# Splitting the second layer's expert weights inside the first layer's expert loop

## The chip, the cores and the metric

One Trainium2 chip, one of its cores. The core has a matrix engine (TensorE, "PE" in the profile; its weight loads are "PEld"), a vector engine (VectorE, "DVE"), an activation engine (ScalarE, "ACT"), a general engine (GpSimd, "POOL") and SyncE ("SP"), which here only issues DMAs. The engines run their own instruction streams and meet through semaphores. The metric is the device time of one execution in microseconds (us), the median of several runs.

## What is computed

A two-layer tower over 8 images: a tokenizer, an attention block with fake quantization, a mixture of 8 experts (top 2), then a second attention block and a second mixture of 8 experts with a shared expert. 2048 tokens of width 192 in all. What matters here are the two expert layers, and of them the weights of the second:

```
def _L1_ffn_ref(x, Wr, W1, b1, W2, b2, sW1, sb1, sW2, sb2):
    logits = xf @ Wr.T
    topv, idx = jax.lax.top_k(logits, K)                      # K = 2 of E = 8
    gates = ...at[arange(T)[:, None], idx].add(softmax(topv))
    h = relu(einsum('td,ehd->teh', xf, W1) + b1)              # W1: 8 experts, 768 x 192
    y = einsum('teh,edh->ted', h, W2) + b2                    # W2: 8 experts, 192 x 768
    moe = einsum('te,ted->td', gates, y)
    return moe + 0.1 * K * (relu(xf @ sW1.T + sb1) @ sW2.T + sb2)
```

The float32 weights are used as two float16 parts, a high one and a low one: high = weight x scale rounded to float16, low = weight x scale - high. Making the two parts of a weight piece is called a split below. The scales are powers of two from the largest absolute weight of a matrix; those of the second layer's expert weights are known before the first expert layer begins.

## The kernel before

The program is a row of blocks; all engines meet at the end of each. Those that matter, in order: the first layer's expert preparation, its expert loop, and then the second attention in four blocks (projection, maxima, context, output), then the second expert layer.

**The expert loop** (`experts`, lines 2193 to 2452) works off 23 slots. A slot is a group of tokens of one expert: 7 small slots of 128 tokens come first, then 16 large slots of 256 (`BIG`, 16; `EARLY`, 7). Each engine has its order written out. In step p, PE does `up` of slot p+1 (L2282, 30 matmuls into `m_pu`), turns the gathered rows of slot p+2 (L2250, into `m_px`), and does `down` of slot p (L2301, 36 matmuls into `m_py`). `down` waits until DVE has made the low part of that slot's hidden values (`lowered`) and has taken the result of the slot before (`out`). ACT does for each slot three GELUs (L2379) and three high parts (L2368). DVE's step p is: copy of the turned rows of slot p+2 (L2404), three low parts of slot p+1 (L2412), result of slot p (L2422). POOL issues the gathers of later slots' rows (L2213) and the adding scatters of the results (L2225), both indirect DMAs. SP issues eight small loads, then waits for the last two scatters and fetches the first quarter of `h` back (`take_back`, L1598), on which the next block's first DVE work waits.

**The splits.** The second layer's expert weights are 16 pieces: for each of the 8 experts one of `w1` (128 x 1536 float32, 768 KB) and one of `w2` (128 x 1152, 576 KB). The class `Halves` (L2606) brings them through SBUF: `fetch` loads a piece into one of 4 places of `hv_raw`, a split makes both parts in one of 3 places of `hv_parts`, `store` writes them to DRAM (`w1h_d`, `w2h_d`), from where the second expert layer loads them (`load_halves`, L1740, which waits for the store of each piece). All of this stands in the second attention:

- Projection block (L2824 to L3068): pieces 0 to 5 (`FRONT`). ACT makes the high part (L2640) and a scaled copy (L2645), POOL subtracts (L2650). They stand in ACT's order ahead of and inside `take(i)`, whose copies (L2969) free the PSUM banks for which PE waits. At the end of the block POOL reduces the shared expert's weight maxima over the partitions (`weigher.reduce`, L193) and DVE computes the scales from it (`weigher.scales`, L201 to L204).
- Maxima block (L3158): nothing of it.
- Context block (L3231 to L3346): pieces 6 to 15. DVE makes both parts (L2657, L2659), two pieces ahead of the first image and one behind each of the 8 images.

## Time and profile before

| | us |
|---|---|
| median of 3 runs | 943.89 (942.99 to 946.34) |
| profiled execution, its own time | 942.19 |
| its span | 940.4 |
| PE busy | 680.5 |
| DVE busy | 655.0 |
| ACT busy | 639.8 |
| POOL busy | 309.9 |

Busy shares over the whole span hide that the stages have different limits, so the profile is read by stretch. The expert loop of the first layer runs from about 410 to 545 us of the span, the projection block from 552 to 614, the maxima block to 650, the context block to 702. In such a table "PEclk" is the clock granted to TensorE as a share of 2.4 GHz, and the DMA share is the mean busy share of the core's 16 DMA engines.

### The profile page before, as it was taken

The page shows a single profiled execution, that of the slowest core. Times are in us where ns is not written, and L with a number is a line of the kernel's source. Part 1 is how long each engine was busy: PE and PEld are TensorE (multiplying, and loading weights), DVE is VectorE, ACT ScalarE, POOL GpSimd, SP SyncE. Part 2 cuts the span into 40 slices and gives each one's busy share as a digit, 9 for nine tenths or more (in the row PEclk, how much of TensorE's full clock was granted, in tenths as well). Part 3 has the DMA queues.
Part 4 walks back from the last instruction along what each step waited for, and adds up shares of the span by engine and source line. Part 5 has one row for each costly group of instructions (what it writes and reads, how often), then busy time and mean ns, then how long its engine had stood idle before and what let it go on. Part 6 is the DMA issues. An engine that isn't in the chain of part 4 may idle for free. (4 is left out here: it accounts for less than half of the span.)

```text
span 940.4 us, 19693 instructions
## 1 busy us (share of the span) xinstructions
PE 680.5 (72%) x7374; PEld 518.0 (55%) x7375; DVE 655.0 (70%) x1370; ACT 639.8 (68%) x1217; POOL 309.9 (33%) x250
## 2 busy tenths in 40 slices
PE   2675472344199655989999937646965898999995
PEld 2553240122077423479999934334544467999994
DVE  3478998999679888855454558667669875554542
ACT  1468955999799686876556427788844752977672
POOL 6730650000000000047887443400001202688754
PEclk9797555555589776999999967955987899999999
DMA  6444772000032224943343365600744942333432
GB/s 200 144 89 116 245 243 61 0 17 9 1 105 100 93 84 141 333 106 68 61 60 54 33 188 190 235 2 28 267 184 159 331 177 73 60 63 61 62 34 30
DMA packets 61478, 106.06 MB, mean 113 GB/s; under 512 B 9725, under 2 KB 43144, under 8 KB 61144
## 3 DMA queue, kind: packets, MB, share of 16 engines
q1 hardware_dynamic: 45016, 88.48, 28.4%
q0 software_dynamic: 16384, 16.53, 11.3%
q8 instruction: 50, 0.82, 0.4%
q14 instruction: 28, 0.23, 0.1%
HBM read 77.20 MB, written 27.77 MB: 112 GB/s over the span
## 5 line engine op out<-in xcount | busy, mean ns | idle before, releaser
L2412 DVE SCALAR_TENSOR_TENSOR m_hT<-m_pu,m_unit,m_hT 128x512 f16<-128x512 f32 (+1 forms) x138 | 86.3, 663 | 21.2 <-ACT m_hT L2368 21.2
L1140 ACT ACTIVATE a_ex<-m_pieces,a_nb 128x256 bf16<-128x256 f16 x192 | 94.3, 492 | 5.4 <-DVE a_nb L1166 5.4
L2404 DVE COPY m_xgT<-m_px 128x768 f16<-128x768 f16 (+1 forms) x46 | 22.9, 497 | 102.6 <-PE m_px L2250 102.6
L2375 ACT ACTIVATE m_pu<-m_pu,m_b,m_unit 128x256 f32<-128x256 f32 (+1 forms) x138 | 63.7, 507 | 44.7 <-PE m_pu L2282 42.7
L979 PE MATMUL a_pp<-a_room 16*128 16x256 bf16 x240 | 56.1, 413 | 40.0 <-DVE m_pieces L1154 31.8
L2368 ACT ACTIVATE m_hT<-m_pu,m_unit 128x512 f16<-128x512 f32 (+1 forms) x138 | 81.3, 634 | 0.0
L2213 POOL DMA_INDIRECT m_xg<-xn_d,m_token x70 | 68.9, 985 | 35.1 <-issue 18.9
L2379 ACT ACTIVATE m_pu<-m_pu,m_unit 128x512 f32<-128x512 f32 (+1 forms) x69 | 41.2, 596 | 52.1 <-PE m_pu L2282 52.1
L2225 POOL DMA_INDIRECT out_h<-m_yo,m_token x39 | 62.1, 1592 | 31.4 <-DVE m_yo L2422 19.6
L2225 POOL DMA_INDIRECT h_d<-m_yo,m_token x39 | 62.1, 1591 | 25.6 <-issue 10.1
L2282 PE MATMUL m_pu<-m_xgT,m_pieces 128*128 128x256 f16 (+1 forms) x690 | 69.4, 260 | 0.9 <-DVE m_xgT L2404 0.9
L2282 PE MATMUL m_pu<-m_xgT,m_w 128*128 128x256 f16 (+1 forms) x690 | 69.1, 259 | 0.9 <-DVE m_xgT L2404 0.9
L979 PEld LDWEIGHTS a_pp<-a_room 16*128 16x128 bf16 x240 | 30.4, 136 | 65.7 <-DVE m_pieces L1154 39.0
L2282 PEld LDWEIGHTS m_pu<-m_xgT,m_pieces 128*128 x690 | 60.0, 100 | 6.8 <-DVE m_xgT L2404 1.2
L2282 PEld LDWEIGHTS m_pu<-m_xgT,m_w 128*128 x690 | 59.7, 99 | 6.8 <-DVE m_xgT L2404 1.3
L2301 PE MATMUL m_py<-m_w,m_hT 128*128 x702 | 63.0, 246 | 0.0
L2301 PE MATMUL m_py<-m_pieces,m_hT 128*128 x702 | 61.7, 246 | 0.9 <-DVE m_yo L2422 0.9
L2301 PEld LDWEIGHTS m_py<-m_w,m_hT 128*128 128x128 f16 x702 | 58.5, 98 | 0.0
L2301 PEld LDWEIGHTS m_py<-m_pieces,m_hT 128*128 128x128 f16 x702 | 57.7, 98 | 1.1 <-issue 1.1
L1154 DVE TENSOR_SCALAR m_pieces<-a_pp,a_sc 128x2048 f16<-128x2048 f32 x24 | 56.3, 2347 | 1.6 <-PEq L988 1.6
L1080 DVE TENSOR_REDUCE a_mxs<-a_pp 128x1 f32<-128x2048 f32 x24 | 53.0, 2283 | 2.2 <-PE a_pp L979 1.6
L1304 ACT ACTIVATE a_e<-a_pt 128x1024 f32<-128x1024 f32 x48 | 49.1, 1024 | 2.8 <-PE a_pt L1250 1.2
(494 smaller groups left out, 1675.6 us busy)
## 6 DMA issues: line engine op xcount, KB each, us to landing
m_pieces<-in_m_w SPq DMA_DIRECT2D x11, 768.0 KB, 5.1
a_early_w<-in_m_w SPq DMA_DIRECT2D x10, 768.0 KB, 5.4
hv_raw<-in_m_w SPq DMA_DIRECT2D x8, 768.0 KB, 7.1
w1h_d<-hv_parts SPq DMA_DIRECT2D x8, 768.0 KB, 4.0
m_w<-w1h_d SPq DMA_DIRECT2D x8, 768.0 KB, 8.7
m_pieces<-in_m_w SPq DMA_DIRECT2D x8, 576.0 KB, 6.1
a_room<-in_m_w SPq DMA_DIRECT2D x8, 576.0 KB
hv_raw<-in_m_w SPq DMA_DIRECT2D x8, 576.0 KB, 6.5
```

The costliest lines, as they stand in the source:

```text
L979: last = nc.tensor.matmul(pp[:, n % 2, j, qt * S:(qt + 1) * S], qkb[:, load % 2, h, qt * P:(qt + 1) * P], qkb[:, load % 2, H + h, :], star ...
L1080: v.tensor_reduce(mxs[:, n:n + 1], pp[:, n % 2], AX.XY, ALU.max, apply_absolute_value=True).then_inc(read, 1)
L1140: last = act.activation(ex[:, n % 2, r], v16t[:, n, r, :], ACT.Exp, bias=nbt[:, n, r:r + 1], scale=scale, accum_out=sumst[:, n, r:r + 1])
L1154: v.tensor_scalar(v16t[:, n], pp[:, n % 2].rearrange("p j (t q) -> p (j t) q", q=S), col["f_s"], HALF, ALU.mult, ALU.add).then_inc(read, 1)
L1304: act.activation(e[:, j], pt[:, j], ACT.Exp, scale=scale).then_inc(raised[j], 1)
L2213: pool.indirect_dma_start(xg[:, x.b, j, :], None, xn_d, bass.IndirectOffsetOnAxis(ap=token[:, n:n + 1], axis=0)).then_inc(got[x.b], 16)
L2225: pool.indirect_dma_start(total_d, bass.IndirectOffsetOnAxis(ap=token[:, n:n + 1], axis=0), yo[:, x.b, j, :], None, compute_op=ALU.add).th ...
L2282: last = nc.tensor.matmul(pu[:, u, q // 2, (q % 2) * w:(q % 2 + 1) * w], w1_bytes[:, bass.ds(e * (2 * W) + up_place(wpart, tail, q), 2 * P ...
L2301: last = nc.tensor.matmul(py[:, j * D:(j + 1) * D], hT[:, u, hpart, q * w + j * P:q * w + (j + 1) * P], w2_bytes[:, bass.ds(e * (2 * FC * ...
L2368: act.activation(hT[:, u, 0, n * 2 * w:(n + 1) * 2 * w], pu[:, u, n, 0:2 * w], ACT.Identity, scale=unit[:, 1:2]).then_inc(hhigh, 1)
L2375: act.activation(pu[:, u, n, q * w:(q + 1) * w], pu[:, u, n, q * w:(q + 1) * w], ACT.Relu, bias=b1[:, bass.ds(e * FC + 2 * n + q, 1)], sca ...
L2412: last = v.scalar_tensor_tensor(hT[:, u, 1, third], pu[:, u, n, 0:2 * w], unit[:, 1:2], hT[:, u, 0, third], ALU.mult, ALU.subtract)
```

## The change

All sixteen pieces are split in the first layer's expert loop by a new class `Ahead`, one behind each of the 16 large slots: ACT makes a high part behind each large slot's `hidden`, DVE the low part behind each large slot's `step`. The piece numbers follow the slots; even pieces are of `w1`, odd ones of `w2`. `Ahead` has one raw place and one place for the parts for each of the two kinds. Its `move` stands in SP's order between the small loads and the wait ahead of `take_back`. `Halves` keeps its code but has no pieces left (`COUNT` is 0), and `load_halves` waits for no store. The shared expert's `weigher.reduce` goes to POOL in the maxima block, and `weigher.scales` to DVE in the same block, behind pair 9 of 11.

```diff
@@ load_halves
-                    prepared.wait_put(sp, 2 * e + down)
+                    if 2 * e + down >= Halves.START:
+                        prepared.wait_put(sp, 2 * e + down - Halves.START)
@@ expert loop: sync, scalar, vector
                     if following:
                         following.load(sp)
+                        ahead.move(sp)
                         for p in (MAXT - 2, MAXT - 1):
                             sp.wait_ge(stored[p % 4], slot(p).landed)
                         take_back(c, total_d, back, sp, 0)
                     with act.Fori(0, BIG // 4) as k:
                         for n in range(4):
                             hidden(in_group(k, n))
+                            if ahead:
+                                ahead.split_high(act, k, n)
                     with dve.Fori(0, BIG // 4 - 1) as k:
                         for n in range(4):
                             step(in_group(k, n), in_group(k, n + 1), in_group(k, n + 2))
-                    steps(EARLY + BIG - 4, MAXT)
+                            if ahead:
+                                ahead.split_low(dve, k, n)
+                    for n in range(4):
+                        steps(EARLY + BIG - 4 + n, EARLY + BIG - 3 + n)
+                        if ahead:
+                            ahead.split_low(dve, BIG // 4 - 1, n)
@@ new
+class Ahead:
+    COUNT = 16
+    def __init__(self, c, a, scratch, ctx):
+        self.raw = c.sb("ah_raw", [P, 2, 2 * FF], F32, ctx)
+        self.parts = c.sb("ah_parts", [P, 2, 2, 2 * FF], F16, ctx)
...
+    def fetch(self, sp, n):
+        down = n % 2
+        if n >= 2:
+            sp.wait_ge(self.put[down], 16 * (n // 2))
+        sp.dma_start(self.tiles(down)[0], self.a["m1_w2" if down else "m1_w1"][n // 2])\
+          .then_inc(self.fetched[down], 16)
+    def store(self, sp, n):
+        down = n % 2
+        sp.wait_ge(self.low[down], n // 2 + 1)
+        sp.dma_start(self.scratch["w2h" if down else "w1h"][n // 2].rearrange("p (r w) -> p r w", r=2),
+                     self.tiles(down)[1]).then_inc(self.put[down], 16)
+    def move(self, sp):
+        for n in range(2):
+            self.fetch(sp, n)
+        for n in range(self.COUNT):
+            self.store(sp, n)
+            if n + 2 < self.COUNT:
+                self.fetch(sp, n + 2)
+        for down in range(2):
+            sp.wait_ge(self.put[down], 16 * (self.COUNT // 2))
+    def split_high(self, act, k, n):
+        act.wait_ge(self.fetched[down], k * 32 + 16 * (n // 2 + 1))
+        act.activation(parts[:, 0, :], raw, ACT.Identity, scale=scale).then_inc(self.high[down], 1)
+    def split_low(self, dve, k, n):
+        dve.wait_ge(self.high[down], k * 2 + (n // 2 + 1))
+        self.c.nc.vector.scalar_tensor_tensor(parts[:, 1, :], raw, scale, parts[:, 0, :], ALU.mult, ALU.subtract)\
+            .then_inc(self.low[down], 1)
@@ Halves
-    COUNT, FRONT, MIXED, RAW, PARTS = 2 * E, 6, 8, 4, 3
+    START = Ahead.COUNT
+    COUNT, FRONT, MIXED, RAW, PARTS = 2 * E - START, 0, 0, 4, 3
@@ projection block: gpsimd, scalar, vector
                         for n in range(Halves.FRONT):
                             halves.low(pool, n)
-                        weigher.reduce(pool)
-                                if z == 3:
-                                    split(2 * i + 1)
-                            split(2 * i)
+                            split(i)
                         weigher.offer(dve)
-                        weigher.scales(dve, link)
@@ maxima block: gpsimd, vector
+                        @block.gpsimd
+                        def _(pool):
+                            weigher.reduce(pool)
                                 quarter(dve, p)
+                                if p == LAST - 2:
+                                    weigher.scales(dve, Chain(dve, scaling).link)
```

Three places show how the instructions stand. First, SP's order in the block of the expert loop, before (`a_wo` is the last of the small loads, `h<-h_d` is `take_back`, then the projection block begins):

```order
L2706 DMA a_room<-in_select 96x1536
L2707 DMA a_wo<-in_bproj 1x192
L1598 DMA h<-h_d 128x4x192
L2196 UNCONDITIONAL_BRANCH
L2826 UNCONDITIONAL_BRANCH
L1598 DMA h<-h_d 128x4x192 x3
L2632 DMA hv_raw<-in_m_w 128x1536
L2632 DMA hv_raw<-in_m_w 128x1152
```

and now (`ah_raw` are the fetches, the writes to `w1h_d` and `w2h_d` the stores):

```order
L2771 DMA a_room<-in_select 96x1536
L2772 DMA a_wo<-in_bproj 1x192
L2636 DMA ah_raw<-in_m_w 128x1536
L2636 DMA ah_raw<-in_m_w 128x1152
L2642 DMA w1h_d<-ah_parts 128x3072
L2636 DMA ah_raw<-in_m_w 128x1536
L2642 DMA w2h_d<-ah_parts 256x1x1152
L2636 DMA ah_raw<-in_m_w 128x1152
L2642 DMA w1h_d<-ah_parts 128x3072
```

The 16 fetches and 16 stores now stand ahead of `take_back`, in strict turn: the store of a piece, then the fetch of the piece two further on.

Second, ACT's order in the loop over large slots, before (one slot and the head of the next; L2379 is the GELU, L2368 the high part of the hidden values):

```order
L2379 ACTIVATE m_pu<-m_pu,m_unit 128x512
L2372 REGISTER_ALU
L2379 ACTIVATE m_pu<-m_pu,m_unit 128x512
L2368 ACTIVATE m_hT<-m_pu,m_unit 128x512
L2372 REGISTER_ALU
L2379 ACTIVATE m_pu<-m_pu,m_unit 128x512
L2368 ACTIVATE m_hT<-m_pu,m_unit 128x512 x2
L2372 ISA
L2379 ACTIVATE m_pu<-m_pu,m_unit 128x512
```

and now:

```order
L2382 ACTIVATE m_pu<-m_pu,m_unit 128x512
L2375 REGISTER_ALU
L2382 ACTIVATE m_pu<-m_pu,m_unit 128x512
L2371 ACTIVATE m_hT<-m_pu,m_unit 128x512
L2375 REGISTER_ALU
L2382 ACTIVATE m_pu<-m_pu,m_unit 128x512
L2371 ACTIVATE m_hT<-m_pu,m_unit 128x512 x2
L2658 ISA
L2659 ACTIVATE ah_parts<-ah_raw,scale 128x1536
L2375 ISA
L2382 ACTIVATE m_pu<-m_pu,m_unit 128x512
```

The high part of a weight piece stands between two slots' hidden values, and whatever it waits for, the next slot's GELUs wait for too.

Third, POOL's order at the end of the projection block, before (L2849 are the last memsets of `a_vv`, L193 the reduction):

```order
L2849 MEMSET a_vv 128x16x4 x3
L2650 ISA
L2650 TENSOR_TENSOR hv_parts<-hv_raw,hv_parts 128x1536
...
L2650 TENSOR_TENSOR hv_parts<-hv_raw,hv_parts 128x1152
L193 ISA
L193 ISA scale<-peak 128x2
L2824 UNCONDITIONAL_BRANCH
```

and now:

```order
L2914 MEMSET a_vv 128x16x4 x3
L2889 UNCONDITIONAL_BRANCH
L3243 UNCONDITIONAL_BRANCH
L193 ISA scale<-peak 128x2
L3220 UNCONDITIONAL_BRANCH
```

The six subtractions are gone, the reduction has moved into the next block, and the separate `ISA` row ahead of it is gone with them.

## Rows read from the trace of the kernel before

**Rows 1.** By stretch: length, busy PE PEld DVE ACT POOL, clock, DMA share, GB/s
```profile
410.50:545.00 134.50, 133.10 (x1534) 126.77 (x1534) 66.57 (x133) 75.34 (x138) 93.23 (x72) 0.99 0.39 63
552.00:614.00 62.00, 38.22 (x224) 21.13 (x224) 44.70 (x91) 39.44 (x58) 24.85 (x14) 0.78 0.63 226
650.30:702.30 52.00, 43.61 (x984) 26.68 (x985) 36.62 (x68) 35.96 (x32) 0.00 (x0) 0.89 0.57 205
```

**Rows 2.** Timeline of a large slot in the loop: start, duration, engine, line, operation
```profile
472.79 3.44 PE L2282 MATMUL m_pu<-m_xgT,m_pieces 128*128 128x256 f16 x30
476.33 0.66 ACT L2379 ACTIVATE m_pu<-m_pu,m_unit 128x512 f32<-128x512 f32 x1
476.90 1.27 ACT L2368 ACTIVATE m_hT<-m_pu,m_unit 128x512 f16<-128x512 f32 x2
477.18 2.06 DVE L2412 SCALAR_TENSOR_TENSOR m_hT<-m_pu,m_unit,m_hT 128x512 f16<-128x512 f32 x3
479.37 0.82 PE L2282 MATMUL m_pu<-m_xgT,m_pieces 128*128 128x256 f16 x6
479.77 0.74 DVE L2422 TENSOR_SCALAR m_yo<-m_py,m_share 128x192 f32<-128x192 f32 x2 [0.54 <-PE m_py L2301]
480.66 0.66 ACT L2379 ACTIVATE m_pu<-m_pu,m_unit 128x512 f32<-128x512 f32 x1 [2.49 <-PE m_pu L2282]
```

**Rows 3.** Instructions that write the parts of a piece: duration ns min/median/max
```profile
L2659 DVE SCALAR_TENSOR_TENSOR hv_parts<-hv_raw,scale,hv_parts x10: 1417/1618/1820, 654.2 to 699.6; 128x1536 f16<-128x1536 f32 x5, 128x1152 f16<-128x1152 f32 x5
L2640 ACT ACTIVATE hv_parts<-hv_raw,scale x6: 1247/1408/1582, 571.0 to 599.4; 128x1536 f16<-128x1536 f32 x3, 128x1152 f16<-128x1152 f32 x3
```

**Rows 4.** DMA issues at 335, 577.5, 669, 687 us: KB, us from issue to landing
```profile
m_pieces<-in_m_w SPq DMA_DIRECT2D x1, 768.0 KB, 4.8
...
w1h_d<-hv_parts SPq DMA_DIRECT2D x1, 768.0 KB, 4.1
hv_raw<-in_m_w SPq DMA_DIRECT2D x1, 768.0 KB, 6.1
...
w1h_d<-hv_parts SPq DMA_DIRECT2D x1, 768.0 KB, 4.3
hv_raw<-in_m_w SPq DMA_DIRECT2D x1, 768.0 KB, 8.1
...
w1h_d<-hv_parts SPq DMA_DIRECT2D x1, 768.0 KB, 3.3
```

**Rows 5.** Timeline of the projection block's first round, ACT and PE
```profile
570.98 1.57 ACT L2640 ACTIVATE hv_parts<-hv_raw,scale 128x1536 f16<-128x1536 f32 x1
574.06 0.67 ACT L2969 ACTIVATE a_qs<-a_pq,a_rowc 128x512 f16<-128x512 f32 x1
575.61 5.33 PE L2891 MATMUL a_pq<-a_xs,a_room 96*96 96x512 f16 x12
```

**Rows 6.** Timeline of the projection block's end, POOL and DVE
```profile
606.93 0.16 DVE L187 TENSOR_REDUCE peak<-peaks 128x2 f32<-128x16 f32 x1
612.28 0.37 POOL L193 PARTITION_ALL_REDUCE scale<-peak  x1 [7.85 <-issue]
613.29 0.17 DVE L204 RECIPROCAL scale<-unscale 128x2 f32<-128x2 f32 x1
```

**Rows 7.** Timeline of the context block's end, PE and DVE
```profile
693.28 0.85 PE L3278 MATMUL a_pc<-a_e,a_vv 128*32 128x256 f32 x12
699.60 1.42 DVE L2659 SCALAR_TENSOR_TENSOR hv_parts<-hv_raw,scale,hv_parts 128x1152 f16<-128x1152 f32 x1
```

**Rows 8.** Busy time by stretch, columns as in Rows 1: TensorE's clock rising and fallen
```profile
566.00:568.00 2.00, 2.00 (x28) 1.50 (x27) 0.98 (x2) 0.59 (x1) 1.36 (x4) 0.71 0.94 383
572.00:574.00 2.00, 0.60 (x2) 0.11 (x2) 1.96 (x4) 1.97 (x2) 0.00 (x0) 0.99 0.01 4
574.00:576.00 2.00, 1.22 (x3) 0.54 (x4) 1.96 (x4) 2.00 (x4) 1.61 (x1) 0.50 0.00 0
```

**Rows 9.** Timeline, DVE and POOL at work together: start, duration
```profile
404.73 1.39 POOL L1730 DMA_INDIRECT m_xg<-xn_d,m_token  x1 [0.30 <-issue]
405.21 3.14 DVE L289 SCALAR_TENSOR_TENSOR m_pieces<-m_early,scale,m_pieces 128x1536 f16<-128x1536 f32 x2
```

More of the change, by code:

```diff
@@ L2192, in experts @@
             pq = pu[:, MAXT % 2]
+            ahead = None if layer else Ahead(c, a, scratch, s1)
             if following:
@@ L2603, in add, with tiles @@
                                             ALU.mult, ALU.add).then_inc(self.added, 1)
+class Ahead:
+    COUNT = 16
+    def __init__(self, c, a, scratch, ctx):
+        self.c, self.a, self.scratch = c, a, scratch
+        self.raw = c.sb("ah_raw", [P, 2, 2 * FF], F32, ctx)
+        self.parts = c.sb("ah_parts", [P, 2, 2, 2 * FF], F16, ctx)
+        self.fetched, self.high, self.low, self.put = (
+            [c.sem(f"ah_{n}{down}") for down in range(2)] for n in ("fetched", "high", "low", "put"))
+    def tiles(self, down):
+        w = Halves.WIDTH[down]
+        return self.raw[:, down, 0:w], self.parts[:, down, :, 0:w], self.c.scale[:, 2 + down:3 + down]
+    def fetch(self, sp, n):
[19 more added lines that the diff above has]
+    def split_high(self, act, k, n):
+        down = n % 2
+        raw, parts, scale = self.tiles(down)
+        act.wait_ge(self.fetched[down], k * 32 + 16 * (n // 2 + 1))
+        act.activation(parts[:, 0, :], raw, ACT.Identity, scale=scale).then_inc(self.high[down], 1)
+    def split_low(self, dve, k, n):
+        down = n % 2
+        raw, parts, scale = self.tiles(down)
+        dve.wait_ge(self.high[down], k * 2 + (n // 2 + 1))
+        self.c.nc.vector.scalar_tensor_tensor(parts[:, 1, :], raw, scale, parts[:, 0, :], ALU.mult, ALU.subtract)\
+            .then_inc(self.low[down], 1)
 class Halves:
     WIDTH = (2 * FF, FC * D)
-    COUNT, FRONT, MIXED, RAW, PARTS = 2 * E, 6, 8, 4, 3
+    START = Ahead.COUNT
+    COUNT, FRONT, MIXED, RAW, PARTS = 2 * E - START, 0, 0, 4, 3
     def __init__(self, c, a, scratch, ctx):
@@ L2631, in fetch @@
             sp.wait_ge(self.lowered, n - self.RAW + 1)
-        sp.dma_start(self.tiles(n)[0], self.a["m1_w2" if n % 2 else "m1_w1"][n // 2])\
+        sp.dma_start(self.tiles(n)[0], self.a["m1_w2" if n % 2 else "m1_w1"][(n + self.START) // 2])\
           .then_inc(self.fetched[n % self.RAW], 16)
@@ L2663, in store @@
         sp.wait_ge(self.lowered, n + 1)
-        sp.dma_start(self.scratch["w2h" if n % 2 else "w1h"][n // 2].rearrange("p (r w) -> p r w", r=2),
+        sp.dma_start(self.scratch["w2h" if n % 2 else "w1h"][(n + self.START) // 2]
+                     .rearrange("p (r w) -> p r w", r=2),
                      self.tiles(n)[1]).then_inc(self.put[n % self.PARTS], 16)
@@ L3152, in attention1 @@
                     TURNS = {16: 0, 17: 2}
+                    scaling = c.sem("a1m_scaling")
                     def beside(n):
```

## The prediction

> **What bounds the kernel now.** I read the busy table by stretch first, since the limits differ by stage [rows 1]. In the expert loop (410 to 545 us) PE is busy 133.1 of 134.5 us at full clock, while ACT has 75.3 and DVE 66.6: PE sets the time, and both engines that get the new work have room. In the projection block (552 to 614) no engine is busy more than 44.7 of 62 us, so it is bound by waits between engines. In the context block (650 to 702) PE has 43.6 of 52, and what it lacks lies at the two ends. Then the timeline of one large slot [rows 2]: PE starts `up` at 472.79 and the next at 479.37, 6.58 us a slot. ACT is done at 478.17 and idles 2.49 us until the next GELU; DVE is done with the slot's result at 480.51 and idles until the next turned rows. Last the DMAs' time from issue to landing [rows 4], because a piece of the new work is no longer only instructions: it needs a fetch and a store.
>
> **The instructions added to the loop: nothing by themselves.** ACT gets 16 high parts, 1.58 us for a `w1` piece and 1.25 for `w2`; DVE gets 16 low parts, 1.82 and 1.42 [rows 3]. Each fits into a hole of its engine (2.49 us on ACT, about 2.7 on DVE) [rows 2]. Were the data always there, the loop would keep 6.58 us a slot. The cost if that cover is gone is what follows.
>
> **The wait added: the main term.** SP fetches piece n+2 only when the store of piece n has landed, the store waits for DVE's low part, and the low part of piece n stands in DVE's order behind the low parts of the *next* slot's hidden values, which ACT makes only after the high part of piece n. So there is a ring for each kind of piece, and it has to go round once in two slots, 13.16 us. Its length for `w1`:
>
> - high part on ACT 1.58 [rows 3]
> - the next slot's six ACT instructions, which by then have their inputs: 0.57 apart and 1.27 for the last two, 3.55 [rows 2]
> - DVE's last low part of these ends 1.07 behind ACT (479.24 against 478.17), then the result, 0.74 [rows 2]
> - DVE's low part of the piece 1.82 [rows 3]
> - store to landing: 3.3 where it ran alone, 4.1 and 4.3 beside other transfers. POOL's indirect DMAs keep the 16 DMA engines 0.39 busy in the loop [rows 1]; I take 3.7
> - fetch to landing: 4.8 at the best, 6.1 beside a store, 8.1 under load. In the loop the odd piece's store will run beside the even piece's fetch, so the nearest row is 6.1; I take 5.9 [rows 4]
>
> Sum 8.8 + 9.6 = 18.4 us, against 13.16. ACT will stand in front of its high part, with the next slot's GELUs queued behind it; DVE's low parts wait for these, PE's `down` for DVE, and POOL's scatters for the results. Pieces 0 and 1 are fetched early, pieces 2 to 15 are seven rounds: 7 x (18.4 - 13.16) = 36.7. The `w2` ring is shorter (smaller pieces), so it hides in the `w1` ring: I expect slots alternating between about 6.6 and 11.8 us. At the end the last low part, 1.42, stands on DVE ahead of the fold's maxima, for which POOL's reduction and then the last scatter wait: +1.4. The last store (3.3 to 4.3) also stands ahead of `take_back` in SP's order, but that waits for POOL's last scatters some 8 us behind the last result, which hides it: 0.
>
> PE now idles some 5 us in each round. The clock was granted at 0.50 in 574 to 576, right behind a stretch with 0.60 of 2 us busy, and it was on its way back in 566 to 568, 0.71, with PE fully busy [rows 8]. Work at 1.2 GHz costs PE up to 2.7 us more per fall, but PE has 5.2 us a round to spare, so most of it is hidden: +2, bounds 0 and +19 (seven falls at 2.7 that nothing hides). The Trainium skill (TensorE: Matmul & The Clock Gate, the part on HAM oscillation) says that waits inside a loop put the clock back each time and that every burst then starts slow; by that the falls come in every round, which the spare time would still cover.
>
> Loop in all: 36.7 + 1.4 + 2 = +40. Bounds: shortest rows 3.3 + 4.8 give a ring of 16.9 and +27; longest 4.3 + 8.1 give 21.2 and +58.
>
> One more thing is queued against POOL: the low parts read two SBUF operands while POOL issues indirect DMAs. Where just this happened before, DVE took 3.14 for two (1.57 each, no more than elsewhere) and POOL's DMA issue 1.39 [rows 9]. So 0. The Trainium skill (SBUF — State Buffer, on the shared port pair) says that an instruction with two SBUF inputs and a GpSimd instruction that reads SBUF exclude each other for their whole length. By that a low part would wait for one of POOL's issues in each round, some 1.4 us and about +10 in all; the trace shows no sign of it on DVE.
>
> **What goes.** In the projection block ACT's first split stood from 570.98 to the copy at 574.06, 3.1 us in front of `take` [rows 5], and PE's next projection at 575.61 waits for the banks that these copies free. DVE's own copies for the same banks would then be the last, so I give back two thirds, 2.1 us, in each of three rounds: 6.2. PE's projection took 5.33 us at the low clock [rows 5]; a shorter gap may spare it one fall: +0.8. Together 7, bounds 0 and 9.4 + 2.6. At its end, DVE's maximum was done at 607.09 and its last scale at 613.46, because POOL's reduction started only at 612.28 with 7.85 us of "issue" in front of it [rows 6]; the block now ends at the maximum. 6.4. In the maxima block four small DVE instructions (0.17 each) are added where DVE waits for ACT: 0.
> In the context block PE's last mixing ended at 694.13, yet DVE still had two splits around the last image and ended at 701.02 [rows 7]. The last image's own copy, turn, reciprocals and product need some 2.1 us, so the block ends 4.8 earlier; bounds 2.2 (only the last split counts) and 6.9. The eight stores and fetches there, and the second layer's wait for the stores, were not late for anything: 0. Gain in all 7 + 6.4 + 4.8 = 18.2; bounds 8.6 and 25.
>
> **Sum.** 942.2 (the profiled execution) + 40 - 18.2 = 964.0. The median of the runs shown is 1.7 above that execution, so 965.7: **966 us**, 2.3% slower.
>
> **Rivals.**
> 1. *The ring takes no time, and only the gains count* (faster). It is one mechanism: the transfers would have to be short enough that the ring closes within the two slots. From 13.16 - 8.8, store and fetch together would need 4.4 us. For it: the engines' holes are wide enough. Against it: the shortest two rows add up to 8.1 [rows 4]. It would give 944 - 18 = 926. The change breaks even where the ring is 13.16 + (18.2 - 3.4) / 7 = 15.3 us, store and fetch 6.5.
> 2. *Transfers under load*. Pieces meet POOL's gathers and scatters and take 4.3 + 8.1, as at 669 us [rows 4]: ring 21.2, loop +58, in all 943.9 + 58 - 18 = 984. For it: DMA share 0.39 before the added 21 MB. Against: before the change the loop moved only 63 GB/s [rows 1], and the 8.1 fell beside other large transfers.
> 3. *The clock stays down.* Against my +2, each fall is paid in full: +19 in place of +2, 983. For it: one gap of 5 us in each round, as long as what stood ahead of the fall in rows 8. Against: PE's spare time in every round.
> 4. *POOL's DMA issues and DVE's low parts wait for each other.* In each of the seven rounds the low part would wait for one issue of 1.39 [rows 9]: +10, 976. For it: both are at work in the same microseconds. Against: the row of DVE in rows 9 is not stretched. The rule of the Trainium skill cited above (SBUF — State Buffer, shared port pair) is this case.
>
> **How the numbers follow.** The forecast (ring of 17.5 to 19.5) has 0.66; rival 2 0.12; rival 3 0.08; rival 4 0.04; rival 1 0.06; in between, a ring of 15 to 16 with large gains, which would end near no change, 0.04. Faster by over 0.3% (which is about what can be told from no change here, 3 us) 0.07, within 0.3% 0.02, slower 0.91. The range leaves out rival 1 and little else: low from the shortest rows with large gains, 943.9 + 27 - 20 = 951; high from the longest with usual gains, 984 to 985. 951 to 985.
>
> **What would show it.** ACT in the loop waits for a DMA into `ah_raw` in front of the high part of every even piece from the second on, 5 us each and some 35 in all; slots alternate; the loop is about 38 to 42 us longer; PE's busy time in it is hardly more. In the timeline of SP each fetch starts where the store before it has landed. The projection block is some 13 us shorter, with no "issue" in front of the reduction on its path, and the context block 5. I am wrong if ACT's wait for `ah_raw` is under 1 us per piece, if store and fetch together take under 7 or over 12 us, or if the projection block is not at least 8 us shorter.

## The result, and the profile after

| | before | after |
|---|---|---|
| median of the runs, us | 941.9 | 944.2 |
| its ratio to before | | 1.003 (95% interval 1.0015 to 1.0044) |
| span of the profiled execution | 940.4 | 943.6 |
| loop: first `up` to the fold's matmuls | 131.9 | 157.4 |
| gap: fold's matmuls to the next block's first turn | 15.6 | 16.2 |
| projection block, to PE's first scores of the next | 56.0 | 39.9 |
| maxima block | 36.2 | 36.0 |
| context block | 52.0 | 45.7 |
| output block | 19.1 | 18.2 |
| second expert layer to the end | 219.0 | 221.6 |

The change makes the kernel 0.3% slower; 966 us were predicted, range 951 to 985. The lower rows are start times of the same PE instructions in the two traces, subtracted. "The fold" is PE's last work in the loop's block, the product of the next attention's weights (`m_pu<-a_pm,a_wa`). Loop and gap grew by 26.0 us and the four blocks behind them shrank by 23.6; besides, the loop began 1.8 us earlier and the second expert layer took 2.6 us longer, and the prediction had neither. So the direction was right and the mechanism too, but the cost was put 14 us too high and the gains 5.4 us too low.

By stretch, as [rows 1] of before: start and end, length, busy PE PEld DVE ACT POOL, clock, DMA share, GB/s.

```profile
408.00:566.00 158.00, 136.18 (x1508) 128.12 (x1509) 88.68 (x144) 95.10 (x155) 102.14 (x72) 0.95 0.69 190
582.00:622.00 40.00, 33.43 (x224) 20.01 (x224) 32.01 (x76) 21.90 (x44) 6.23 (x6) 0.87 0.10 37
658.00:704.00 46.00, 43.21 (x986) 26.88 (x987) 13.03 (x48) 35.95 (x32) 0.00 (x0) 0.94 0.02 4
```

PE has about the same work in the loop as before (136 against 133 us) but stands still for 22 us of it. What it waits for is in the waits of 430 to 570 us: engine, tile and line waited for, us in total, times, longest.

```profile
ACT ah_parts L2659 <- DMA ah_raw<-in_m_w: 48.1, 14, 6.5
DVE m_hT L2417 <- ACT m_hT L2371: 42.6, 25, 7.0
...
PE m_py L2304 <- DVE m_yo L2427: 20.9, 7, 8.3
POOL h_d L2228 <- DVE m_yo L2427: 17.6, 4, 5.8
```

The chain can be read downwards: ACT waits for the fetch, DVE for ACT, PE's `down` for DVE, POOL's scatter for the result. This is the predicted wait at the predicted place. One turn of the `w1` ring in the timeline (start, duration, engine, line, operation, idle before):

```profile
471.05 1.58 ACT L2659 ACTIVATE ah_parts<-ah_raw,scale 128x1536 f16<-128x1536 f32 x1 [5.60 <-DMA ah_raw<-in_m_w]
...
474.81 1.28 ACT L2371 ACTIVATE m_hT<-m_pu,m_unit 128x512 f16<-128x512 f32 x2
475.55 1.41 DVE L2417 SCALAR_TENSOR_TENSOR m_hT<-m_pu,m_unit,m_hT 128x512 f16<-128x512 f32 x2 [0.41 <-ACT m_hT L2371]
...
476.87 0.73 DVE L2427 TENSOR_SCALAR m_yo<-m_py,m_share 128x192 f32<-128x192 f32 x2
...
477.52 1.81 DVE L2665 SCALAR_TENSOR_TENSOR ah_parts<-ah_raw,scale,ah_parts 128x1536 f16<-128x1536 f32 x1
...
479.36 0.33 SPq L2642 DMA_DIRECT2D w1h_d<-ah_parts  x1
...
482.70 0.33 SPq L2636 DMA_DIRECT2D ah_raw<-in_m_w  x1
...
487.41 1.58 ACT L2659 ACTIVATE ah_parts<-ah_raw,scale 128x1536 f16<-128x1536 f32 x1 [5.38 <-DMA ah_raw<-in_m_w]
```

High part to store issue 8.31 us, store issue to fetch issue 3.34, fetch issue to the next high part 4.71: 16.36, the shortest of the seven rings. The eight high parts of `w1` start at 436.6, 454.5, 471.1, 487.4, 503.9, 520.5, 537.2 and 554.8. The first ring is 17.9 us; the six behind 454.5 have a mean of 16.7, made of 8.3 + 3.4 + 5.05. All seven take 118.2 us, 26.1 over the 92.1 of seven times two slots. The prediction had 8.8 + 3.7 + 5.9 = 18.4.

The clock fell with PE's waits, though not in every round (stretches as in [rows 1]):

```profile
478.00:486.00 8.00, 8.00 (x92) 7.67 (x91) 6.40 (x9) 4.04 (x7) 6.16 (x5) 1.00 0.80 228
486.00:494.00 8.00, 5.07 (x54) 4.52 (x51) 2.85 (x6) 6.14 (x8) 5.21 (x4) 0.95 0.80 236
494.00:502.00 8.00, 7.89 (x56) 7.18 (x56) 6.04 (x8) 3.61 (x7) 6.55 (x4) 0.62 0.69 176
```

Two more such stretches stand at 526 (0.79) and 558 us (0.57), where the clock was at 1.2 GHz for a part of the time; in the others it was 0.95 and more, that is 2.4 GHz for all or nearly all of it. PE waited seven times in the loop (20.9 us in all), four of them for 3 us or more. The clock fell in or right behind the waits of 3.04 us (to 494.1), 3.35 (to 527.2) and 8.25 (to 561.5), and did not fall in or behind that of 3.15 (to 477.75) or the three shorter ones. The Trainium skill (TensorE: Matmul & The Clock Gate, HAM oscillation) has the clock go back with each wait in a loop; here it went back in three rounds of seven.

In the projection block ACT's splits are gone from in front of `take`, and the reduction stands where nothing waits for it. The same two instructions as in [rows 6]:

```profile
621.15 0.16 DVE L187 TENSOR_REDUCE peak<-peaks 128x2 f32<-128x16 f32 x1
622.19 0.37 POOL L193 PARTITION_ALL_REDUCE scale<-peak  x1 [30.53 <-POOLq L2889]
```

PE's first scores of the next block follow the maximum's end by 0.86 us; before it was 6.97. At the end of the context block, against [rows 7], DVE now follows PE:

```profile
700.60 0.85 PE L3346 MATMUL a_pc<-a_e,a_vv 128*32 128x256 f32 x12
...
702.82 0.42 DVE L3408 TENSOR_TENSOR a_cx<-a_pc,a_inv 128x96 f32<-128x96 f32 x2
```

### The profile page after: what moved, and what is told of

Read it like the earlier page. It is cut to its first block and busy times, and to the rows that moved or that the text cites. A ratio compares the mean times of both kernels' runs of the same rounds, so it can differ in the third digit from the quotient of the medians.

```text
span 943.6 us, 19686 instructions
## 1 busy us (share of the span) xinstructions
PE 678.8 (72%) x7374; PEld 518.7 (55%) x7375; DVE 646.6 (69%) x1366; ACT 643.5 (68%) x1221; POOL 302.1 (32%) x244
## 3 DMA queue, kind: packets, MB, share of 16 engines
q1 hardware_dynamic: 45016, 88.48, 28.4%
## 5 line engine op out<-in xcount | busy, mean ns | idle before, releaser
L2216 POOL DMA_INDIRECT m_xg<-xn_d,m_token x70 | 72.0, 1029 | 33.7 <-issue 19.5
L2304 PE MATMUL m_py<-m_pieces,m_hT 128*128 x702 | 67.7, 259 | 20.9 <-DVE m_yo L2427 20.9
L2228 POOL DMA_INDIRECT h_d<-m_yo,m_token x39 | 68.1, 1745 | 43.1 <-DVE m_yo L2427 19.2
L2304 PEld LDWEIGHTS m_py<-m_pieces,m_hT 128*128 128x128 f16 x702 | 62.6, 103 | 22.8 <-DVE m_hT L2417 21.6
L2659 ACT ACTIVATE ah_parts<-ah_raw,scale 128x1536 f16<-128x1536 f32 (+1 forms) x16 | 22.7, 1418 | 48.1 <-DMA ah_raw<-in_m_w 48.1
```

The source lines that it names most:

```text
L2216: pool.indirect_dma_start(xg[:, x.b, j, :], None, xn_d, bass.IndirectOffsetOnAxis(ap=token[:, n:n + 1], axis=0)).then_inc(got[x.b], 16)
L2228: pool.indirect_dma_start(total_d, bass.IndirectOffsetOnAxis(ap=token[:, n:n + 1], axis=0), yo[:, x.b, j, :], None, compute_op=ALU.add).th ...
L2304: last = nc.tensor.matmul(py[:, j * D:(j + 1) * D], hT[:, u, hpart, q * w + j * P:q * w + (j + 1) * P], w2_bytes[:, bass.ds(e * (2 * FC * ...
```

## The experiments

Each ratio is to the runs of before on the same chip. "Stretch" is how much longer POOL's DMA issues of 430 to 600 us took than 1.58 us (scatter) or 0.98 us (gather), summed over those that exceed it by over 0.15 us. "Landing" is how long POOL waited, between 435 and 530 us and ahead of its scatters, for an earlier scatter to land. Loop and gap are those of the one profiled execution; the loop of "only the reduction moved" is the code of before and took 1.5 us less, so differences of that size in the loop say nothing.

| kernel | median | ratio, 95% | loop | gap | stretch | landing |
|---|---|---|---|---|---|---|
| before | 941.9 | | 131.9 | 15.6 | 0 | 5.5 |
| after | 944.2 | 1.003, 1.0015 to 1.0044 | 157.4 | 16.2 | 9.1 | 7.0 |
| low part first | 940.0 | 0.999, 0.9965 to 1.0011 | 135.8 | 33.8 | 11.0 | 8.1 |
| no fetch | 921.0 | 0.979, 0.9757 to 0.9821 | 130.5 | 19.3 | 2.9 | 8.5 |
| together | 939.8 | 0.998, 0.9949 to 1.0012 | 143.7 | 16.1 | 5.4 | 11.8 |
| double fetch | 985.9 | 1.048, 1.0449 to 1.0518 | 198.1 | 16.2 | 12.0 | 5.0 |
| two pieces | 920.0 | 0.978, 0.9749 to 0.9813 | 132.0 | 15.7 | 1.2 | 8.0 |
| low first, no fetch | 926.3 | 0.986, 0.9811 to 0.9906 | 132.4 | 24.5 | 4.9 | 9.5 |
| low first, one input | 933.6 | 0.993, 0.9907 to 0.995 | 138.0 | 22.0 | 4.0 | 8.5 |
| low first, tiny | 936.2 | 0.993, 0.9895 to 0.9966 | 142.9 | 24.0 | 0 | 19.1 |
| eight pieces | 930.8 | 0.990, 0.9866 to 0.9931 | 130.7 | 28.4 | 4.7 | 11.6 |
| six pieces | 934.2 | 0.993, 0.9896 to 0.9959 | 132.1 | 23.8 | 4.1 | 10.2 |
| eight pieces, in halves | 928.3 | 0.986, 0.9826 to 0.9885 | 131.9 | 24.1 | 3.8 | 8.4 |
| only the reduction moved | 936.4 | 0.993, 0.9896 to 0.9955 | 130.4 | 15.7 | 0 | 6.2 |

### The ring: its length against the loop's

**Double fetch** (a longer ring):

```
             if n + 2 < self.COUNT:
                 self.fetch(sp, n + 2)
+                if n % 2 == 0:
+                    sp.wait_ge(self.fetched[0], 32 * (n // 2 + 1))
+                    self.fetch(sp, n + 2)
...
-        act.wait_ge(self.fetched[down], k * 32 + 16 * (n // 2 + 1))
+        act.wait_ge(self.fetched[down], k * (64, 32)[down] + (32 * (n // 2) + 16, 16 * (n // 2 + 1))[down])
```

> As the changed kernel, but each even piece from piece 2 on is fetched twice, the second time when the first has landed. Ring theory: the ring grows by one fetch, 4.7 to 5.5 us with its issue, to about 21.5 us, seven times: +33 to +38, 977 to 983 us; PE then stands still for 8 us in each round, and its busy time says whether the clock falls there. Rival (traffic or instructions set the loop's length): 7 fetches more of 28 transfers, +6, 950.

Measured 985.9, 3 us above the range given. The high parts of `w1` start 22.4 us apart (461.44 to 595.64 in six rings), 5.65 more than after. All seven rings take 158.7 us, 40.4 more than after's 118.2, and the loop is 40.8 us longer. So the loop follows the ring by a factor of seven. TensorE's clock fell in each of the five rounds between 478 and 590 us, in waits of PE of 5.4 to 7.4 us (0.52 to 0.75 over the 8 us in which it worked again, that is 1.2 GHz for part of them), yet of these 40.8 us all but 0.4 are the ring. The falls were hidden in PE's spare time, as the prediction's clock step had it, and rival 3, which paid them in full, is out.

**Together** (a shorter ring, by letting store and fetch run at once):

```
-            sp.wait_ge(self.put[down], 16 * (n // 2))
+            sp.wait_ge(self.low[down], n // 2)
...
-                     self.tiles(down)[1]).then_inc(self.put[down], 16)
+                     self.tiles(down)[1]).then_inc(self.fetched[down], 16)
...
-        act.wait_ge(self.fetched[down], k * 32 + 16 * (n // 2 + 1))
+        act.wait_ge(self.fetched[down], k * 64 + 16 * (n // 2 * 2 + 1))
```

> The fetch of piece n+2 waits for the low part of piece n, not for its store; store and fetch go out together, and the high part waits for both. The ring is then 8.3 + the later landing of the two. Theory (transfers that are alone run at 3.3 and 4.7; together they share what the DMA engines moved in the loop, 232 GB/s, so 1.5 MB take 6.6): ring 14.9, loop 144, 932 to 936. If the two do not hinder each other, the later is the fetch with 5: ring 13.3, loop 133, 919 to 921. Rival (traffic in itself costs): 944.

The first line changed is the wait ahead of the fetch of piece n; the other two let the high part wait for store and fetch. Runs from 931.4 to 943.7, median 939.8, 4 us above the range of the shared-transfers case; the profiled one is the fastest of them. In it the ring is 14.8 us and the loop 143.7, as that case had it:

```profile
518.39 1.81 DVE L2665 SCALAR_TENSOR_TENSOR ah_parts<-ah_raw,scale,ah_parts 128x1536 f16<-128x1536 f32 x1
520.23 0.33 SPq L2642 DMA_DIRECT2D w1h_d<-ah_parts  x1
520.60 0.43 SPq L2636 DMA_DIRECT2D ah_raw<-in_m_w  x1
...
526.33 1.58 ACT L2659 ACTIVATE ah_parts<-ah_raw,scale 128x1536 f16<-128x1536 f32 x1 [4.49 <-DMA ah_raw<-in_m_w]
```

Here store and fetch do meet, and from the store's issue to the next high part it takes 6.1 us. In the changed kernel the two transfers of one ring run one after the other, and only the odd piece's store falls into the even piece's fetch. Why most other runs of this kernel were 5 to 12 us slower wasn't traced.

**No fetch** (the ring without its fetch; all 32 instructions stay):

```
-                     self.tiles(down)[1]).then_inc(self.put[down], 16)
+                     self.tiles(down)[1]).then_inc(self.fetched[down], 16)
...
         for n in range(self.COUNT):
             self.store(sp, n)
-            if n + 2 < self.COUNT:
-                self.fetch(sp, n + 2)
...
-            sp.wait_ge(self.put[down], 16 * (self.COUNT // 2))
+            sp.wait_ge(self.fetched[down], 16 * (self.COUNT // 2 + 1))
```

> Pieces 0 and 1 alone are fetched; all 16 splits and stores are made, from those two pieces again and again, and a high part waits for the store before. Left out: the loading of 14 pieces. Theory of the ring: 8.3 + store 3.3 = 11.6 us, under 13.16, so no wait: the loop is back at 132 to 134 us, 917 to 922. Rival, the instructions themselves cost: 944. Rival, the traffic costs in proportion to the bytes: half of it is left, about 932.

Measured 921.0. ACT waited 7.5 and 3.7 us in all for the stores, and no longer for a fetch. So the added instructions and stores cost the loop nothing that shows (130.5 us), as the prediction's first term said, and the loop's 25 us are the wait.

**Two pieces** (nothing of the other fourteen in the loop):

```
+                    if ahead:                       # ACT, ahead of the large slots
+                        for n in range(2):
+                            ahead.split_high(act, 0, n)
...
-        for n in range(self.COUNT):
+        for n in range(self.DONE):                  # 2
```

> Only pieces 0 and 1 are split, ahead of the large slots, and the second expert layer loads these two for every expert. Left out: the other 14 pieces' fetch, split and store. It measures the gains of the other blocks by themselves. By the ring: the loop is as before, 131.9 us plus at most 3 for the two splits, and the time 917 to 921 (944.2 - 25.5, and up to 3 more). What it differs by from the kernel with the low part first is the price of 14 pieces' instructions and transfers where nothing waits for them: theory under 2 us, rival (instructions or traffic cost) over 8.

The second expert layer loads these two for every expert. Measured 920.0. This is what the gains alone are worth: 22 us under before.

Summed over the seven rounds, the rings exceed seven times 13.16 us by 12.2 (together), 26.1 (after) and 66.5 (double fetch), and the loops exceed that of before by 11.8, 25.5 and 66.2. Where the ring is under 13.16 (no fetch) or not there (two pieces), the loop is 130.5 and 132.0.

### The limit behind the ring: POOL

**Low part first** (the ring cut to 12.3 us on paper, nothing left out):

```
-                            step(in_group(k, n), in_group(k, n + 1), in_group(k, n + 2))
                             if ahead:
                                 ahead.split_low(dve, k, n)
+                            step(in_group(k, n), in_group(k, n + 1), in_group(k, n + 2))
...
```

> DVE's low part of a piece stands ahead of the step it stood behind; nothing else differs from the changed kernel. Theory (the ring sets the loop: high part, six ACT instructions, DVE's lag, result, low part = 8.3 us, then store 3.3 and fetch 4.7 = 16.3 against 13.16): the low part now follows its high part by one result, so the engines' share falls from 8.3 to about 4.2 and the ring to about 12.3 us, under two slots. ACT's wait for ah_raw goes from 48 us to under 5, the loop from 157 back to 132 to 134 us, the time to 917 to 922. Rival (the 32 instructions and 28 transfers themselves cost the 25 us, through engines, DMA engines or SBUF ports): the order of one DVE instruction changes nothing, 944.

Both expectations were wrong. The ring is gone, ACT's wait for `ah_raw` fell from 48.1 us to 0.7, and PE's loop is back to within 4 us. But the time is 940, near the 944 of the rival, whose mechanism it isn't. The waits of 430 to 570 us in this kernel:

```profile
POOL h_d L2228 <- DMA h_d<-m_yo,m_token: 24.9, 11, 3.7
...
ACT a_room L2795 <- DVE a_wsc L2820: 17.1, 1, 17.1
DVE a_wsc L2817 <- POOL a_wsc L2802: 14.9, 1, 14.9
```

and its timeline behind the loop:

```profile
548.70 2.21 PE L2781 MATMUL m_pu<-a_pm,a_wa 96*96 96x96 f32 x24
...
558.29 1.55 POOL L2228 DMA_INDIRECT h_d<-m_yo,m_token  x1 [2.74 <-DMA h_d<-m_yo,m_token]
560.15 1.55 POOL L2228 DMA_INDIRECT h_d<-m_yo,m_token  x1 [0.30 <-issue]
564.43 1.55 POOL L2228 DMA_INDIRECT h_d<-m_yo,m_token  x1 [2.73 <-DMA h_d<-m_yo,m_token]
...
567.30 0.90 POOL L2802 PARTITION_ALL_REDUCE a_wsc<-a_top  x1
...
582.53 1.94 PE L2927 MATMUL a_pt<-ident,a_xn 128*96 128x128 f32 x8 [30.97 <-DVE a_xn L3078]
```

PE is done at 551, but POOL still has scatters to issue, each pair 6.14 us behind the last because it waits for the landing of the one before. Weight scales, `take_back` and the next block stand behind them: the gap is 33.8 us in place of 15.6. POOL had no room from the start. Its rows of the kernel before, 435 to 530 us (busy, mean ns of one, idle before):

```profile
L2225 POOL DMA_INDIRECT h_d<-m_yo,m_token x29 | 46.2, 1595 | 16.2 <-issue 7.7 <-DMA h_d<-m_yo,m_token 5.5 <-DVE m_yo L2422 3.0
L2213 POOL DMA_INDIRECT m_xg<-xn_d,m_token x26 | 25.8, 992 | 7.9 <-issue 7.6 <-PE m_px L2250 0.3
```

Two scatters, two gathers and 0.30 us of issue in front of each make 2 x 1.595 + 2 x 0.992 + 4 x 0.30 = 6.37 us of the slot's 6.58. What lengthens POOL's work by over 0.2 us a slot comes out at the loop's end. In the changed kernel the slow ring hid this.

What lengthens it was taken apart by three kernels, all with the low part first.

**Low first, no fetch** (the edits of both):

> The low part ahead of the step, and pieces 0 and 1 alone are fetched. Left out: the loading of 14 pieces. With the low part ahead of the step PE's loop was as before the change, yet POOL fell behind with its scatters and the next block began 26 us late. Two causes are told apart. Port: POOL's DMA issues (mean 1.91 against 1.60 us a scatter, 1.12 against 0.99 a gather) are stretched by DVE's low parts, which read two SBUF operands; these are all still here, so POOL is still behind: 935 to 942. Traffic: scatters land later (up to 7.1 against 3.8 us) because 1.5 MB more move in two slots; half of that is gone: 919 to 924.

**Low first, one input:**

```
-        self.c.nc.vector.scalar_tensor_tensor(parts[:, 1, :], raw, scale, parts[:, 0, :], ALU.mult, ALU.subtract)\
+        self.c.nc.vector.tensor_scalar(parts[:, 1, :], raw, scale, None, ALU.mult)\
...
```

> The low part ahead of the step, but DVE writes it from one SBUF operand (a scaled copy of the raw piece; left out: the subtraction of the high part). All fetches and stores are made. Port: POOL's issues are back at 1.60 and 0.99 to 1.05 us and POOL keeps up: 919 to 924. Traffic: scatters land as late as with two operands, POOL stays behind: 935 to 942.

**Low first, tiny** (behind a clearing of the parts' places, once, ahead of the loop):

```
-        self.c.nc.vector.scalar_tensor_tensor(parts[:, 1, :], raw, scale, parts[:, 0, :], ALU.mult, ALU.subtract)\
+        self.c.nc.vector.scalar_tensor_tensor(parts[:, 1, 0:8], raw[:, 0:8], scale, parts[:, 0, 0:8], ALU.mult, ALU.subtract)\
```

> The low part ahead of the step, all fetches and stores made, but DVE's low part writes 8 columns only (the rest of it is zeros, set once ahead of the loop; left out: the subtraction elsewhere). In all runs so far each POOL issue that was stretched by over 0.15 us overlapped a low part; here there is nothing left to overlap with, and the whole traffic of 28 transfers remains. Port alone: POOL keeps up, 919 to 924. Traffic alone: as with the low part first, 938 to 942. Both, as the two half removals say (fetches gone 926, one operand in half the time 934): POOL's issues at 1.60 and 0.99 but waits for landing of 12 us or more, 928 to 934.

926.3, 933.6 and 936.2: none gives the 919 to 924 of a single cause, and the third is 2 us above the range for both. In the rows both causes are seen. The low part is one. In all eleven kernels with whole low parts, every issue that was stretched by over 0.15 us overlapped a low part of DVE, as here with the low part first:

```profile
443.69 1.82 DVE L2665 SCALAR_TENSOR_TENSOR ah_parts<-ah_raw,scale,ah_parts 128x1536 f16<-128x1536 f32 x1 [0.21 <-ACT ah_parts L2659]
443.90 3.10 POOL L2228 DMA_INDIRECT h_d<-m_yo,m_token  x1 [0.30 <-issue]
```

The low part ends at 445.51 and the issue 1.49 us later, about its usual length: it was as if it began then. The order of the two decides. In the ten kernels whose low parts read two operands, 78 low parts began while an issue of POOL was under way; every one kept its length (1.41 or 1.82 us at most), and so did the issues. DVE's own mean stayed at 1.61 us. With one input the low part is shorter (0.93 us) and the stretch smaller but not gone (4.0); tiny, it is 0. The Trainium skill (SBUF — State Buffer, on the shared port pair) says that whoever starts first holds the pair for its whole instruction; by that POOL is the one to be blocked where the low part came first, and the trace agrees. By the same rule the low part would wait where POOL came first, and there the traces don't agree, as the 78 low parts show. The Trainium skill names two-input instructions and those in a two-port mode; that the one-input low part was in such a mode no row here shows.

The traffic is the other cause. In the tiny kernel POOL's issues have their old length and yet it waits, 19.1 us for landings against 5.5 before:

```profile
L2228 POOL DMA_INDIRECT h_d<-m_yo,m_token x24 | 38.5, 1603 | 25.1 <-DMA h_d<-m_yo,m_token 19.1 <-issue 3.7 <-DVE m_yo L2427 2.3
L2216 POOL DMA_INDIRECT m_xg<-xn_d,m_token x26 | 25.8, 993 | 7.9 <-issue 7.3 <-PE m_px L2253 0.6
```

A scatter there lands after 5.3 us at the median, against 3.6 before; in the kernel with the stores but without the fetches (no fetch) it is 3.5. The pieces meet it too: ACT waited 28.6 us for `ah_raw` in this kernel, so its loop is 142.9 us and not 132. How much of the low-first kernel's 20 us over the two-piece kernel is port and how much traffic can't be said from these: the parts don't add up, since a late POOL also moves the collisions. A low part ahead of the step also delays DVE's result of that slot, for which the scatter waits, by its own length; the one-input and tiny versions shorten that delay together with the stretch, and no run parts the two.

### Versions meant to be faster

**Eight pieces** in the loop, behind every second large slot; the other eight in the context block, none behind the last two images:

```
-                            if ahead:
-                                ahead.split_high(act, k, n)
+                            if ahead and n % 2 == 0:
+                                ahead.split_high(act, k, n // 2)
...
-    COUNT = 16
+    COUNT = 8
-    COUNT, FRONT, MIXED, RAW, PARTS = 2 * E - START, 0, 0, 4, 3
+    COUNT, FRONT, MIXED, RAW, PARTS = 2 * E - START, 0, 2, 4, 3
```

> Only pieces 0 to 7 are split in the loop, one behind every second large slot (low part behind the step, as in the changed kernel); pieces 8 to 15 are split by DVE in the context block, two ahead of the first image and one behind each of the images 0 to 5. A ring of 16.4 us then has four slots, 26.3 us, to go round in, and POOL's scatters meet half the traffic. Theory (ring, and POOL's queue as the second limit, busy 6.3 of 6.58 us a slot before the change): no wait for ah_raw, a loop of 132 to 134 us, no queue behind POOL, context block still 46 us: 918 to 924. Rival (traffic costs in proportion): 932. This is the version meant to beat both kernels.

930.8: faster than before and after, but 7 us over the range and near the 932 of the rival (traffic costs in proportion). The loop is 130.7 us and no wait for `ah_raw` is left; the gap, 28.4 us, is what was missed. POOL's last two scatters go out at 559.0 and 560.9 us, 16 us behind PE's first matmul of the fold (542.65), in pairs 6.0 to 6.1 us apart.

**Six pieces** (`COUNT = 6`, `MIXED = 3`, none behind the last four slots):

> As the version with half the pieces in the loop, but six of them, behind every second of the first twelve large slots; the other ten in the context block, three ahead of the first image and one behind each of the images 0 to 6. POOL's delay at the end of the loop was 13 us with eight pieces (gap to the next block 28.4 against 15.7 us with none). If it comes piece by piece: about 10 us, less what the split behind image 6 costs (0 to 2): 926 to 931. If POOL catches up in the last four slots: 921 to 924.

934.2, a miss, 3 us above the range. The gap is 23.8, but the context block is back to 51.6 us from 46.5. Either the split behind image 6 or the third one ahead of the first image costs as much as the last two did; which was not tried.

**Eight pieces, in halves** (each fetch and store as two, one after the other):

```
...
+        half = Halves.WIDTH[down] // 2
+        for i in range(2):
+            if i:
+                sp.wait_ge(self.fetched[down], 32 * (n // 2) + 16)
+            sp.dma_start(self.tiles(down)[0][:, i * half:(i + 1) * half],
...
```

> As the version with eight pieces in the loop (930.8 us), but each fetch and each store goes out in two halves, the second when the first has landed, so that no more than 384 KB stand in front of POOL's gathers and scatters at a time; the bytes are the same. If what delays the scatters is the length of a burst: fewer waits of POOL for a landing (11.6 us in 435 to 530 there, 5.5 before the change), 922 to 927. If it is the bytes or the low parts alone: 929 to 933, and more where the second half comes too late for its high part.

928.3, between the two cases, and against before 0.986 (0.9826 to 0.9885). POOL's landing waits fell to 8.4 and the gap to 24.1 us. It is the fastest version that computes everything: 1.4% under before. Against the whole pieces the medians differ by 2.5 us, and the intervals of the two ratios overlap.

**Only the reduction moved**, in the kernel before:

```
-                        weigher.reduce(pool)                  # projection block, POOL
-                        weigher.scales(dve, link)             # projection block, DVE
+                            weigher.reduce(pool)              # maxima block, POOL
+                                if p == LAST - 2:
+                                    weigher.scales(dve, Chain(dve, scaling).link)
```

> The kernel before with only the shared expert's reduction and scales moved to the maxima block; all sixteen splits stay in the second attention. Theory: POOL's reduction stood at the end of the projection block with 7.85 us of issue in front of it and DVE's scales behind, so the block ends at DVE's maximum: -6.4 us, 934.5 to 937. Rival: the 7.85 us belonged to POOL's change from subtractions to the reduction and come back in the maxima block, where nothing waits for them: the same number, so what tells them apart is the reduction's row there. Rival: the block's end is then set by something else (the copies or PE): -2 or less, 940 or more.

936.4, ratio 0.993 (0.9896 to 0.9955), within the range. PE's first scores follow DVE's maximum by 0.87 us in place of 6.97, so 6.1 us are the reduction's. In the maxima block the reduction starts at 613.74 with 10.56 us of "issue" in front of it, so that time came along, as the first rival had it, and nothing waits for it there. The projection block itself is only 3.8 us shorter in this trace; the stretch up to the maximum took 2.3 us longer, which has no part of the edit in it.

This run also says what the versions above owe to the moved reduction, which they all contain: 0.7% of the 1.0 to 1.4%. The interval of the eight whole pieces (0.9866 to 0.9931) overlaps that of the reduction alone, so a gain from its splits isn't shown; that of the halves (0.9826 to 0.9885) lies below it. Six pieces, at 0.993, show no gain over the reduction alone.

## Why the prediction was wrong

Its place, its order and its sign were right: ACT stands in front of the even pieces' high parts, slots alternate, and the cost is seven times what the ring is over 13.16. It failed in sizes.

- **The mis-sized term was the transfers' share of the ring, "I take 3.7" and "I take 5.9".** Measured from issue to what it releases, over the six rings behind 454.5, they are 3.4 and 5.05: 8.4 in place of 9.6 (over all eight rounds the stores of `w1` landed after 3.3 us at the median, its fetches after 5.0). The allowance was for the odd piece's store beside the even piece's fetch and for POOL's indirect DMAs. The overlap is there, as the prediction said: the odd store begins some 2 to 3 us after the fetch (484.90 against 482.70 in the timeline above) and shares 1.5 to 3.6 us with it in every round. But it was priced too high. Six of the seven fetches landed after 4.7 to 5.05 us, by the 4.8 "at the best" of [rows 4], and only the last took 5.9; the 6.1 of the row beside a store was not the price of this overlap. The even stores ran by themselves and took 3.3 to 3.4. Where the transfers were made to start together ("together"), they took 6.1 us for both.
- **The engines' share** was 8.3, not 8.8: each part a tenth or two shorter than in [rows 2].
- With both the ring is 16.7, so 7 x 3.56 = 24.9 in place of 36.7 (26.1 with the longer first ring). Since a ring's excess counts seven times, an error of 1.7 us in 18.4 became 12.
- **Clock, +2.** It fell in three rounds, yet the loop grew by 25.5 us and the seven rings account for 26.1. That the falls are hidden was right; the double fetch shows it with a fall in five rounds out of five. The 2.7 us a fall stood without its rows; the twelve matmuls of the projection took 5.33 us at 1.2 GHz [rows 5] and 2.76 at 2.4 GHz in the same block of before, 2.6 apart.
- **Tail, +1.4.** The gap grew by 0.6.
- **Instructions at nothing:** right for the loop's length (no fetch: 130.5 us). But the cost was put only on ACT and DVE. The prediction weighed POOL against DVE (rival 4) and looked at the stretch on the wrong engine. In [rows 9], its evidence for nothing, POOL's issue began first (404.73 against 405.21), the order in which no low part of two operands and no issue beside it was stretched in any run (with one operand, one gather at 488.62 took 1.42 us). And it had POOL's load only as 93.2 of 134.5 us in [rows 1]. With the issue time in front of each instruction it is 6.37 of 6.58 us. In the changed kernel this cost nothing in the loop's length, since the ring left POOL time, and the gap grew by only 0.6; with the low part first it is the limit, and the other versions with low parts in the loop and no long ring have gaps of 19 to 28 us.
- **Gains, 18.2 predicted, 23.6 measured.** The reduction 6.4: 6.1. The splits in the projection block 7: about 10 (the block is 16.1 shorter); the copies' delay was cut by a third for DVE's copies, and that third seems not to have been needed. That this is the whole of it was not tried apart. Context block 4.8: 6.4. Output block 0: 0.8.
- **The second expert layer** took 221.6 us and not 219.0. The other kernels have either value too: no fetch, together, double fetch and one input 221.3 to 222.1, the remaining eight 218.7 to 219.7. No edit divides them so; its cause stays open.
- **The break-even** of rival 1, a ring of 15.3 us, holds: 16.7 is 1.4 above it, seven times that is 9.8, less 5.4 for the larger gains and 2.2 for tail and clock (0.6 for each, what loop and gap have over 24.9, and not 3.4) leaves 2.2, against 26.0 - 23.6 = 2.4 measured. The median of before over all runs, 941.9, is 2 us under the one that the sum was made from.
- **The sign and the range.** The sign came out right by 2.3 us. That is less than the second expert layer's 2.6 us, which is unexplained, so there is luck in it. The range's low end, 951, paired the shortest ring (+27) with gains of 20; with the prediction's own upper bound for the gains, 25, it would have been 946.

## What to carry to other kernels

A wait that closes a ring (fetch, use, store, fetch) is priced as ring length less the time it has, times the rounds, and an error in one transfer counts once a round. So look in the order of issue for which transfers overlap and for how long: here a store that began 2 to 3 us into a fetch cost it 0.2 us at the median over the shortest row, and not the 1.3 of the row beside another transfer. Before work is moved into a loop, add up every engine's slot with the issue time between its instructions, the engine that only issues DMAs too: it may be the second limit right behind the first. Work moved into such a loop can be dosed: with eight of the sixteen pieces the kernel was 1.0 to 1.4% faster than before, and with all sixteen slower. And when a change has several parts, run each alone: 0.7% came from the reduction, which has nothing to do with the loop.

## What the runs showed of the hardware

- DVE's low part over two SBUF operands held up an indirect DMA issue of POOL that began behind it until it ended (3.10 us against 1.58). In the other order neither was held up (78 low parts of at most 1.82 us).
- 768 KB fetches and stores of SyncE's queue beside POOL's scatters moved the scatters' landing from 3.6 to 5.3 us at the median; with the stores alone it was 3.5. The stores themselves took 3.3 to 3.4 us alone, and the fetches 4.7 to 5.9 us with a 576 KB store beside a part of each.
- TensorE's clock fell from 2.4 to 1.2 GHz in or right behind two of PE's three waits of 3.0 to 3.4 us and in that of 8.25 us, with none of the three under 2 us (after), and in each of five waits of 5.4 to 7.4 us (double fetch).
